# A scan with two feed-forward layers beside it: input spread between the halves of a piece, tanh ahead of bank copies, step sizes taken one tick later

## The chip, the cores and the metric

One core of a Trainium2 chip runs one program. Its engines are TensorE (PE, matmuls into PSUM), VectorE (DVE), ScalarE (ACT), GpSimd (POOL) and SyncE (SP, which here only issues DMAs). Each works through its own instructions in order and waits for the others by semaphores. The metric is the device time of one execution in microseconds, the median of several runs.

## What is computed

Four residual blocks over x of 2 x 1024 tokens and 512 features, each followed by a layer norm: linear attention, a gated feed-forward layer (with a Walsh-Hadamard transform that is folded into its second weight), a selective scan, and a second gated feed-forward layer.

```python
x = _layernorm(x + attention(x))
x = _layernorm(x + ffn0(x))          # silu(x W1) * (x W3), fwht, W2; hidden size 2048
# scan: b = 4 tiles of 512 tokens in the kernel's terms, two tiles per sequence
deltaBC = einsum('bld,od->blo', x, W_bc)          # rank 64, B 32, C 32
delta = softplus(einsum('blr,dr->bld', dt_r, W_dt) + b_dt)
h = exp(delta_t * A) * h + (delta_t * u_t) * B_t  # 512 features x 32 states
y_t = einsum('bdn,bn->bd', h, C_t);  y = y + u * D_param
x = _layernorm(x + y)
x = _layernorm(x + (silu(x Wg) * (x Wu)) Wd)      # hidden size 2048
```

## The kernel before

x stays in SBUF, features on partitions, in four tiles of 512 tokens. After the attention phase one function, `trunk_phase`, does everything else. The time axis is a count of **ticks**, from -24 to 792, that all engines walk through in their own loops (`for tick in range(FIRST_TICK, LAST_TICK)`). The same tick on two engines is not the same moment: an engine is as far as its semaphores let it be. Tables of ticks at module level say what happens in which tick.

**Feed-forward work.** Each tick has one *piece* for PE, in two halves of three matmuls (three-pass fp32: lines 84, 85, 86), `ffn(tick, 0)` and `ffn(tick, 1)`. A unit of 24 ticks makes four chunks of the hidden layer: gate (2 ticks), up (2 ticks), and the second matmul of the unit before, *down*, at ticks 2, 3, 6, 7, 10, 11, 14, 15 of the unit. One tick after a gate has ended (ticks 2, 10, 18 and 22 of a unit) ACT makes tanh of it (L1459) and DVE the silu (L1636); one tick after an up has ended DVE makes the product (L1642, "hidden"), and ACT and POOL split it one tick later into a high and a low part (L1463, L1762). Down accumulates over two ticks in PSUM bank `y_or_aux`; DVE adds it to x in the next tick (L1648).

**The scan.** 512 steps are spread over the 530 ticks from 124 to 653, one a tick (18 ticks have none). A step holds 4 features x 32 states on the 128 partitions, over 512 tokens. For step s: PE spreads delta*x from 32 rows over 128 partitions (L1386, `du_spread`, two PSUM buffers); DVE multiplies it with B (L1679, `d_b`); ACT makes `decay` = exp(delta*A) (L1553); DVE scans (L1699, `h_states`); POOL multiplies with C (L1796); PE sums the states every fourth step (L1395, `scan_y`). Every fourth step's product with B is done by POOL instead, from a copy that ACT makes (L1561, `du_copied`). In tick s DVE scans s and then makes d_b of s+1; ACT makes decay of s+1, which needs the scan of s-1; PE's spread of s+1 opens the tick and needs the d_b two steps back.

**The shared bank.** `y_or_aux` also holds what the layer norms need (mean and variance, in parts and in full), and three things of the scan's preparation for each token tile t: rank (L1340), four *dt* projections (L1351, one for each 128 features, m = 0 to 3) and two *states* matmuls (L1347, for B and C). `bank_turn(tick, half)` issues them between the pieces. The bank goes from user to user in a fixed order (`TURN`): a user waits until its predecessor's result was taken out, by ACT (a copy, or for dt an Abs and a Relu, L1524 and L1525, `dt_take`) or by DVE (the add). For tiles 1 to 3 dt comes at ticks 221, 225, 229, 233 (and 317..., 413...), that is ticks 5, 9, 13 and 17 of a unit. After the fourth, ACT makes the softplus of all four in one go (`soft`: Exp, table load, Ln, table load, L1530 to L1534), in tick 234 (330, 426).

In each tick ACT does, in this order: `copy_input` if due, decay, the bank copies that are due, tanh, h_high, and then the rest (carry, squares, splits, softplus).

## Time and profile before

| | |
|---|---|
| time, median of 3 runs | 1928.1 us (1927.26 to 1929.54) |
| profiled execution, its own time | 1931.71 us |
| its span, first to last instruction | 1929.9 us |
| mean granted TensorE clock | 0.982 |
| PE busy | 1781.0 us (92%) |
| DVE busy | 1336.6 us (69%) |
| POOL busy | 1276.2 us (66%) |
| ACT busy | 988.4 us (51%) |

The attention phase lies ahead of the trunk; the scan takes from about 584 us to 1741 us, and feed-forward work alone fills the rest. A busy share over the whole span mixes these stages, so it is read by stretches. The profile's waits name an engine, the line that waited, and what released it. A matmul's row shows 0.39 us or more, but matmuls are pipelined: in a full stream one starts every 0.23 us.

### The profile page before, as it was taken

The page shows a single profiled execution, that of the slowest core. Times are in us where ns is not written, and L with a number is a line of the kernel's source. Part 1 is how long each engine was busy: PE and PEld are TensorE (multiplying, and loading weights), DVE is VectorE, ACT ScalarE, POOL GpSimd, SP SyncE. Part 2 cuts the span into 40 slices and gives each one's busy share as a digit, 9 for nine tenths or more (in the row PEclk, how much of TensorE's full clock was granted, in tenths as well). Part 3 has the DMA queues.
Part 4 walks back from the last instruction along what each step waited for, and adds up shares of the span by engine and source line. Part 5 has one row for each costly group of instructions (what it writes and reads, how often), then busy time and mean ns, then how long its engine had stood idle before and what let it go on. Part 6 is the DMA issues. An engine that isn't in the chain of part 4 may idle for free. (4 is left out here: it accounts for less than half of the span.)

```text
span 1929.9 us, 27715 instructions
## 1 busy us (share of the span) xinstructions
PE 1781.0 (92%) x9472; PEld 1140.3 (59%) x9472; DVE 1336.6 (69%) x1665; ACT 988.4 (51%) x1671; POOL 1276.2 (66%) x987
## 2 busy tenths in 40 slices
PE   7898998679998999999899899998999999999998
PEld 5666666447855556555455455554556555566886
DVE  2525244232228999889998999889999999994222
ACT  5444342465455656565566455565665555443212
POOL 4533542137518998879887988789988898893111
PEclk9999999889999999999999999999999999999999
DMA  7342332358947888678677887667788677774653
GB/s 240 127 142 72 121 117 82 134 197 291 327 137 276 304 269 295 229 256 282 223 264 240 269 270 254 219 241 254 247 275 276 236 259 260 274 252 145 207 193 99
DMA packets 159292, 427.37 MB, mean 221 GB/s; under 512 B 30992, under 2 KB 54160, under 8 KB 158768
## 3 DMA queue, kind: packets, MB, share of 16 engines
q1 hardware_dynamic: 159152, 425.60, 65.6%
q8 instruction: 76, 1.25, 0.3%
q14 instruction: 64, 0.52, 0.1%
HBM read 356.34 MB, written 69.21 MB: 220 GB/s over the span
## 5 line engine op out<-in xcount | busy, mean ns | idle before, releaser
L1796 POOL TENSOR_TENSOR h_times_c<-h_states,c_rep 128x512 f32<-128x512 f32 x512 | 666.8, 1316 | 115.3 <-DVE h_states L1699 69.6
L1553 ACT ACTIVATE decay<-delta_on_states,a_neg 128x512 f32<-128x512 f32 x512 | 353.5, 692 | 364.6 <-DVE h_states L1699 339.1
L1762 POOL TENSOR_TENSOR h_lo<-silu_in_h_lo,h_hi 128x512 fp32r<-128x512 f32 x128 | 167.2, 1306 | 209.7 <-ACT h_hi L1463 209.1
L1679 DVE TENSOR_TENSOR d_b<-du_spread,b_rep 128x512 f32<-128x512 f32 x384 | 256.7, 668 | 24.4 <-PE du_spread L1386 23.5
L84 PE MATMUL gate<-x_hi,w 128*128 128x512 f32 x512 | 245.7, 480 | 16.4 <-DVE w L1631 6.9
L1699 DVE TENSOR_TENSOR_SCAN h_states<-decay,h_last,d_b 128x512 f32<-128x512 f32 x192 | 245.6, 1279 | 9.2 <-ACT decay L1553 2.3
L1699 DVE TENSOR_TENSOR_SCAN h_states<-decay,d_b 128x512 f32<-128x512 f32 x192 | 234.0, 1219 | 18.0 <-ACT decay L1553 11.8
L84 PE MATMUL up<-x_hi,w 128*128 128x512 f32 x512 | 241.4, 472 | 1.4 <-DVE silu_in_h_lo L1642 1.4
L1386 PE MATMUL du_spread<-stack,selectors 96*128 96x512 bf16 x512 | 201.5, 394 | 43.1 <-DVE d_b L1679 32.3
L84 PE MATMUL y_or_aux<-h_hi,w 128*128 128x512 f32 x468 | 221.0, 472 | 8.6 <-POOL h_lo L1762 6.7
L1636 DVE SCALAR_TENSOR_TENSOR silu_in_h_lo<-silu_in_h_lo,gate 128x512 f32<-128x512 f32 x128 | 87.1, 680 | 172.0 <-ACT silu_in_h_lo L1459 171.9
L85 PE MATMUL gate<-x_lo,w 128*128 128x512 f32 x512 | 203.3, 397 | 0.0
L86 PE MATMUL gate<-x_hi,w 128*128 128x512 f32 x512 | 202.8, 396 | 0.0
L85 PE MATMUL up<-x_lo,w 128*128 128x512 f32 x512 | 202.4, 395 | 0.0
L86 PE MATMUL up<-x_hi,w 128*128 128x512 f32 x512 | 201.6, 394 | 0.0
L85 PE MATMUL y_or_aux<-h_lo,w 128*128 128x512 f32 x468 | 184.4, 394 | 0.0
L86 PE MATMUL y_or_aux<-h_hi,w 128*128 128x512 f32 x468 | 184.0, 393 | 0.0
L1787 POOL TENSOR_TENSOR d_b_by_pool<-du_copied,b_rep 128x512 f32<-128x512 f32 x128 | 168.8, 1319 | 4.0 <-ACT du_copied L1561 4.0
L1386 PEld LDWEIGHTS du_spread<-stack,selectors 96*128 96x128 bf16 x512 | 49.6, 97 | 190.1 <-issue 121.4
L84 PEld LDWEIGHTS gate<-x_hi,w 128*128 128x128 f32 x512 | 99.4, 194 | 94.5 <-issue 69.9
L84 PEld LDWEIGHTS up<-x_hi,w 128*128 128x128 f32 x512 | 99.1, 193 | 75.3 <-issue 63.2
L1395 PE MATMUL scan_y<-h_times_c,sum_selectors 128*32 128x512 f32 x1024 | 139.7, 618 | 1.1 <-POOL h_times_c L1796 1.1
(221 smaller groups left out, 3134.8 us busy)
## 6 DMA issues: line engine op xcount, KB each, us to landing
w<-w_split SPq DMA_DIRECT2D x336, 512.0 KB, 4.3
delta_on_states<-delta SPq DMA_DIRECT2D x256, 512.0 KB, 5.5
w_split<-w_presplit_hi_lo SPq DMA_DIRECT2D x32, 512.0 KB, 3.3
w_split<-w SPq DMA_DIRECT2D x16, 1024.0 KB, 7.3
w_presplit_hi_lo<-in_w13b SPq DMA_DIRECT2D x32, 256.0 KB, 3.6
h_times_c<-in_w13a SPq DMA_DIRECT2D x16, 512.0 KB, 4.4
w_split<-w_presplit SPq DMA_DIRECT2D x16, 512.0 KB, 5.3
delta_x_parts<-delta_x_parts_out SPq DMA_DIRECT2D x16, 384.0 KB, 4.9
```

Of the source, the lines that this page charges most:

```text
L84: pe.matmul(out, w_hi, x_hi, start=first, stop=False)
L85: pe.matmul(out, w_hi, x_lo, start=False, stop=False)
L86: return pe.matmul(out, w_lo, x_hi, start=False, stop=last)
L1386: pe.matmul(uu[:, i % NU], sel[:, r, :], stk[:, o % 2, j]).then_inc(s_uu, 1)
L1395: mm = pe.matmul(yb[j * 32:(j + 1) * 32, :], ysel[:, r, :], hc[:, (s + j) % NC_], start=(r == 0), stop=(r == QB - 1), skip_group_check=Tru ...
L1553: act.activation(da[:, s % ND], dring[:, s % NR], ACT.Exp, scale=a[:, column(s):column(s) + 1]).then_inc(s_da, 1)
L1636: dve.scalar_tensor_tensor(out=sg[:, idx % RH], in0=sg[:, idx % RH], scalar=1.0, in1=gate[:, :], op0=ALU.add, op1=ALU.mult).then_inc(s_sg, 1)
L1679: dve.tensor_tensor(db[:, by_dve(s) % NB], uu[:, i % NU], brep[:, tile_of(s // SPO) % 2], ALU.mult).then_inc(s_db, 1)
L1699: dve.tensor_tensor_scan(hs[:, s % NH], da[:, s % ND], data, initial, ALU.mult, ALU.add).then_inc(s_hs, 1)
L1762: pool.tensor_tensor(hl[:, idx % RH], sg[:, idx % RH], hh[:, idx % RH].bitcast(F32), ALU.subtract).then_inc(s_hl, 1)
L1787: pool.tensor_tensor(dp[:, quad % 2], us[:, :], brep[:, tile_of(JB * quad // SPO) % 2], ALU.mult).then_inc(s_dp, 1)
L1796: pool.tensor_tensor(hc[:, s % NC_], hs[:, s % NH], crep[:, tile_of(s // SPO) % 2], ALU.mult).then_inc(s_hc, 1)
```

## The change

Three edits. The spread of delta*x is issued between the two halves of PE's piece, for step s+2 instead of s+1, and so stands half a tick earlier against the scan. On ACT, tanh and h_high stand ahead of the bank copies of the same tick. For tiles 1 to 3 the Abs and Relu that take a dt out of the bank are done one tick after the dt matmul (`DT_TAKE_AT`), and the two states matmuls are one tick later (235 and 237 instead of 234 and 236, and likewise for tiles 2 and 3). PE's dt matmuls, the softplus and everything on DVE, POOL and SP keep their ticks.

```diff
-STATES_TICK = ((112, 114), (234, 236), (330, 332), (426, 428))
+STATES_TICK = ((112, 114), (235, 237), (331, 333), (427, 429))
...
+DT_TAKE_AT = {tick + (key[0] > 0): key for tick, key in DT_AT.items()}
...
                     if s == -1:
                         spread_input(BY_POOL)
                         spread_input(JB + BY_POOL)
-                    if 0 <= s + 1 < STEPS and (s + 1) % JB != BY_POOL:
-                        spread_input(s + 1)
-                    if 0 <= s and s % JB == 2 and s + 2 * JB + 1 < STEPS:
-                        spread_input(s + 2 * JB + 1)
+                        spread_input(0)
                     bank_turn(tick, 0)
                     ffn(tick, 0)
+                    if -1 <= s < STEPS - 2 and (s + 2) % JB != BY_POOL:
+                        spread_input(s + 2)
+                    if s >= -1 and (s + 1) % JB == 2 and s + 2 * JB + 2 < STEPS:
+                        spread_input(s + 2 * JB + 2)
                     bank_turn(tick, 1)
...
                     if 0 <= s + 1 < STEPS:
                         decay(s + 1)
+                    if tick in TANH_AT:
+                        tanh(TANH_AT[tick])
+                    if tick in H_SPLIT_AT:
+                        h_high(H_SPLIT_AT[tick])
                     if tick in MEAN_PARTS_AT:
                         mean_parts(MEAN_PARTS_AT[tick])
...
-                    if tick in DT_AT:
-                        dt_take(*DT_AT[tick])
-                    if tick in TANH_AT:
-                        tanh(TANH_AT[tick])
-                    if tick in H_SPLIT_AT:
-                        h_high(H_SPLIT_AT[tick])
+                    if tick in DT_TAKE_AT:
+                        dt_take(*DT_TAKE_AT[tick])
```

PE around the second dt of tile 1 (ticks 225 and 226; du_spread is the spread, `y_or_aux<-h_hi` the down piece in the bank that dt used). Before:

```order
2463 L1351 MATMUL y_or_aux<-mean_or_rank,w_dt 128x512 [waits bank_taken0]
2464 L84 MATMUL gate<-x_hi,w 128x512
...
2467 L84 MATMUL gate<-x_hi,w 128x512
...
2470 L1386 MATMUL du_spread<-stack,selectors 128x512 [waits scan_db]
2471 L84 MATMUL y_or_aux<-h_hi,w 128x512 [waits w2_in2,bank_taken0]
...
2474 L84 MATMUL y_or_aux<-h_hi,w 128x512
```

and changed:

```order
2463 L1352 MATMUL y_or_aux<-mean_or_rank,w_dt 128x512 [waits bank_taken0]
2464 L84 MATMUL gate<-x_hi,w 128x512
...
2467 L1387 MATMUL du_spread<-stack,selectors 128x512 [waits scan_db]
2468 L84 MATMUL gate<-x_hi,w 128x512
...
2471 L84 MATMUL y_or_aux<-h_hi,w 128x512 [waits w2_in2,bank_taken0]
...
2474 L1387 MATMUL du_spread<-stack,selectors 128x512 [waits scan_db]
```

The spread moved from the head of the tick to its middle; the lines 85 and 86 that complete each half are left out. The wait of the down piece for the bank stands where it stood.

ACT at the same place, before (soft_in_x_hi and delta_in_x_lo are what the take writes, silu_in_h_lo is tanh):

```order
571 L1553 ACTIVATE decay<-delta_on_states,a_neg 128x512 [waits scan_h,delta_on_states1_in]
572 L1524 ACTIVATE soft_in_x_hi<-y_or_aux,scan_feat 128x512 [waits prep_dt_mm]
573 L1525 ACTIVATE delta_in_x_lo<-y_or_aux,scan_feat 128x512
574 L1553 ACTIVATE decay<-delta_on_states,a_neg 128x512 [waits scan_h]
575 L1459 ACTIVATE silu_in_h_lo<-gate 128x512 [waits y_done,gate_done]
```

and changed:

```order
571 L1555 ACTIVATE decay<-delta_on_states,a_neg 128x512 [waits scan_h,delta_on_states1_in]
572 L1555 ACTIVATE decay<-delta_on_states,a_neg 128x512 [waits scan_h]
573 L1461 ACTIVATE silu_in_h_lo<-gate 128x512 [waits y_done,gate_done]
574 L1526 ACTIVATE soft_in_x_hi<-y_or_aux,scan_feat 128x512 [waits prep_dt_mm]
575 L1527 ACTIVATE delta_in_x_lo<-y_or_aux,scan_feat 128x512
```

The take moved behind the next decay and the tanh. ACT at the fourth dt of tile 1, before:

```order
594 L1553 ACTIVATE decay<-delta_on_states,a_neg 128x512 [waits scan_h,delta_on_states2_in]
595 L1524 ACTIVATE soft_in_x_hi<-y_or_aux,scan_feat 128x512 [waits prep_dt_mm]
596 L1525 ACTIVATE delta_in_x_lo<-y_or_aux,scan_feat 128x512
597 L1553 ACTIVATE decay<-delta_on_states,a_neg 128x512 [waits scan_h]
598 L1518 COPY b_rep<-y_or_aux 128x512 [waits prep_states_mm]
599 L1459 ACTIVATE silu_in_h_lo<-gate 128x512 [waits y_done,gate_done]
600 L1565 COPY h_last<-h_states 128x2 [waits scan_h]
601 L1530 ACTIVATE soft_in_x_hi<-soft_in_x_hi 128x2048 [waits prep_abs]
```

and changed:

```order
595 L1555 ACTIVATE decay<-delta_on_states,a_neg 128x512 [waits scan_h]
596 L1461 ACTIVATE silu_in_h_lo<-gate 128x512 [waits y_done,gate_done]
597 L1526 ACTIVATE soft_in_x_hi<-y_or_aux,scan_feat 128x512 [waits prep_dt_mm]
598 L1527 ACTIVATE delta_in_x_lo<-y_or_aux,scan_feat 128x512
599 L1567 COPY h_last<-h_states 128x2 [waits scan_h]
600 L1532 ACTIVATE soft_in_x_hi<-soft_in_x_hi 128x2048 [waits prep_abs]
601 L1533 ACT_TABLE_LOAD
602 L1535 ACTIVATE soft_in_x_hi<-soft_in_x_hi 128x2048 [waits prep_exp]
603 L1536 ACT_TABLE_LOAD
604 L1563 COPY du_copied<-du_spread 128x512 [waits scan_db_by_pool,scan_du_spread]
605 L1555 ACTIVATE decay<-delta_on_states,a_neg 128x512 [waits scan_h,delta_on_states0_in]
606 L1520 COPY b_rep<-y_or_aux 128x512 [waits prep_states_mm]
```

The take stands behind tanh and right ahead of the softplus, and the copy of b_rep moved from ahead of the softplus to behind it.

## Rows read from the trace of the kernel before

**Rows 1.** By stretches: length, busy PE, PEld, DVE, ACT, POOL (instructions), clock, DMA, GB/s.

```profile
787.00:834.00 47.00, 41.98 (x161) 22.54 (x161) 35.52 (x44) 31.22 (x53) 33.25 (x27) 0.93 0.63 210
...
1269.00:1740.00 471.00, 448.86 (x2058) 265.22 (x2057) 456.10 (x531) 259.23 (x448) 416.74 (x325) 1.00 0.77 259
```

**Rows 2.** Waits of DVE, 577 to 1740 us: total, times, longest.

```profile
DVE silu_in_h_lo L1636 <- ACT silu_in_h_lo L1459: 28.2, 19, 10.2
DVE d_b L1679 <- PE du_spread L1386: 23.5, 31, 1.8
DVE h_states L1699 <- ACT decay L1553: 15.4, 10, 5.2
```

**Rows 3.** Waits of PE, same stretch.

```profile
PE du_spread L1386 <- DVE d_b L1679: 32.3, 35, 3.8
```

**Rows 4.** Waits of DVE, 787:834, 1011:1053, 1227:1269; then PE's, 787:817.

```profile
DVE d_b L1679 <- PE du_spread L1386: 2.5, 3, 1.1
...
DVE d_b L1679 <- PE du_spread L1386: 4.1, 6, 1.4
...
DVE d_b L1679 <- PE du_spread L1386: 5.1, 6, 1.2
...
PE y_or_aux L1351 <- DVE x L1648: 1.3, 1, 1.3
```

**Rows 5.** Timeline at the second dt, PE and then ACT: start, duration, what, [idle before].

```profile
797.24 1.12 PE L1351 MATMUL y_or_aux<-mean_or_rank,w_dt 64*128 64x512 f32 x2
...
799.56 0.39 PE L86 MATMUL gate<-x_hi,w 128*128 128x512 f32 x1
799.79 0.39 PE L1386 MATMUL du_spread<-stack,selectors 96*128 96x512 bf16 x1
799.83 0.59 PE L84 MATMUL y_or_aux<-h_hi,w 128*128 128x512 f32 x1
...
798.40 0.69 ACT L1524 ACTIVATE soft_in_x_hi<-y_or_aux,scan_feat 128x512 f32<-128x512 f32 x1 [2.71 <-PE y_or_aux L1351]
798.99 0.68 ACT L1525 ACTIVATE delta_in_x_lo<-y_or_aux,scan_feat 128x512 f32<-128x512 f32 x1
```

**Rows 6.** Timeline at the first dt, DVE and then PE.

```profile
788.16 1.22 DVE L1699 TENSOR_TENSOR_SCAN h_states<-decay,d_b 128x512 f32<-128x512 f32 x1
...
790.90 0.58 PE L84 MATMUL y_or_aux<-h_hi,w 128*128 128x512 f32 x1
```

**Rows 7.** Timeline at the softplus, by engine; last, stretch 827 to 830 us as in rows 1.

```profile
817.65 0.39 PE L1386 MATMUL du_spread<-stack,selectors 96*128 96x512 bf16 x1
...
820.19 1.93 ACT L1530 ACTIVATE soft_in_x_hi<-soft_in_x_hi 128x2048 f32<-128x2048 f32 x1
...
827.13 1.31 ACT L1553 ACTIVATE decay<-delta_on_states,a_neg 128x512 f32<-128x512 f32 x2
...
827.86 1.22 DVE L1699 TENSOR_TENSOR_SCAN h_states<-decay,d_b 128x512 f32<-128x512 f32 x1 [5.20 <-ACT decay L1553]
...
827.29 0.61 PE L1386 MATMUL du_spread<-stack,selectors 96*128 96x512 bf16 x1 [3.77 <-ACT du_copied L1561]
...
827.00:830.00 3.00, 2.71 (x4) 0.77 (x5) 2.14 (x3) 1.50 (x4) 2.10 (x2) 0.50 0.00 0
```

**Rows 8.** Timeline at the longest wait for a spread, DVE and then ACT.

```profile
1502.96 0.69 DVE L1679 TENSOR_TENSOR d_b<-du_spread,b_rep 128x512 f32<-128x512 f32 x1 [1.79 <-PE du_spread L1386]
1503.57 0.68 DVE L1636 SCALAR_TENSOR_TENSOR silu_in_h_lo<-silu_in_h_lo,gate 128x512 f32<-128x512 f32 x1
...
1502.75 0.60 ACT L1459 ACTIVATE silu_in_h_lo<-gate 128x512 f32<-128x512 f32 x1
```

**Rows 9.** Timeline where a variance copy stands ahead of tanh, ACT and then DVE.

```profile
1202.00 0.60 ACT L1479 ACTIVATE rstd<-y_or_aux 128x512 f32<-128x512 f32 x1 [1.34 <-PE y_or_aux L1326]
1202.50 0.59 ACT L1459 ACTIVATE silu_in_h_lo<-gate 128x512 f32<-128x512 f32 x1
...
1203.12 0.69 DVE L1636 SCALAR_TENSOR_TENSOR silu_in_h_lo<-silu_in_h_lo,gate 128x512 f32<-128x512 f32 x1 [0.71 <-ACT silu_in_h_lo L1459]
```

## The prediction

> **What bounds the kernel now.** I read the table by stretches first. The scan of the third layer fills 577 to 1740 us. From 1269 to 1740 us VectorE (DVE) is busy for 456.1 of 471 us and TensorE (PE) for 448.9 at full clock [rows 1]: two engines, each nearly full, and whichever is late makes the other wait. The stretch 787 to 834 us is different: DVE is busy for only 35.5 of 47 us there. It is one of three stretches (787 to 834, 1011 to 1053, 1227 to 1269) in which the step sizes of the next token tile are made.
>
> Then the waits. Over the stage DVE waits 23.5 us for du_spread in 31 places, 28.2 us for tanh (10.2 of it in one piece before the first scan) and 15.4 us for decay [rows 2]. PE waits 32.3 us for d_b in 35 places [rows 3], since du_spread has two buffers. Of the 23.5 us, the three stretches hold 2.5 + 4.1 + 5.1 = 11.7 us [rows 4], which leaves 11.8 us for the rest of the scan.
>
> Then one tick inside a size stretch, in the timeline. The projection to step sizes (dt, L1351) starts at 797.24, both halves of a gate piece follow, and at 799.83 PE starts a down piece into the same PSUM bank, y_or_aux. That works because ScalarE (ACT) emptied the bank at 798.40 and 798.99, at once [rows 5]. From 787 to 817 us PE has one wait, 1.3 us [rows 4], so PE is the bound between the four dt of a tile. The softplus behind the fourth holds ACT from 820.19, and DVE sits for 5.20 us until decay can follow it at 827.13 [rows 7]. So in a size stretch the chain is PE, dt, ACT, softplus, decay, scan; whatever delays the fourth take delays the scan.
>
> **The change, part by part.** The kernel's profiled execution took 1931.71 us for a span of 1929.9 us; the median of the runs is 1928.1. I work out differences from the profile and add them to the median.
>
> *Step sizes taken a tick behind (tiles 1 to 3).* Abs and Relu of a dt now stand behind the next tick's decay, and after tanh where that tick has one. PE's down piece of that next tick still needs the bank. This concerns three of four dt of a tile (m = 0, 1, 2, ticks 221, 225, 229 and the like); the fourth has no down piece right behind it.
> - m = 0: the scan at 788.16 lasts 1.22, so decay can start at 789.5, Abs and Relu each 0.6 behind (the spacing of 798.40 and 798.99 [rows 5]), Relu lasts 0.68, and PE is let go near 791.5. It went at 790.90 [rows 6]. Cost 0.6 us.
> - m = 1: this tick has a tanh, which needs the gate piece that PE is just ending. Its last matmul starts at 799.56 and is over when the next starts, about 0.23 later. The spread now lies inside the piece, so the gate ends 0.25 later (a tick's spread moved forward, not added). Tanh near 800.2, Abs 800.8, Relu 801.4, bank free near 802.1, against 799.83 [rows 5]. Cost 2.3 us, in which PE has nothing it may start.
> - m = 2: PE is 2.9 us behind by then, and DVE not, so decay is early and the take is done in time. Cost 0.
> - m = 3: taken behind a tanh and a decay, but the copy of b_rep leaves the queue ahead of the softplus. The gate piece ended at 817.65, where the next spread starts, and now ends near 817.65 + 2.9 + 0.25 = 820.8; tanh, Abs and Relu at 0.6 each put Exp near 822.7, where it was at 820.19 [rows 7]. So the softplus, and the scan behind it, is 2.5 us later.
>
> The takes wait less for PE, since dt is done when ACT comes to it, but DVE waits in these stretches for PE and for the softplus, so ACT's own waits bring nothing. The 11.7 us that DVE waits for du_spread there don't count as a gain either: what it wins, it waits at the softplus. Three tiles at 2.5 us: **+7.5 us**. Bounds: 0 if the PE time given up is made good before the fourth dt, 3 x 3.5 = 10.5 if m = 2 costs too.
>
> Here the Trainium skill (Perfetto Trace Analysis, Matmuls under Optimizing Tensor Performance) speaks against the change: matmul groups should rotate through banks so that the emptying of one overlaps the matmuls of the next. Here dt and down share one bank, and the change lengthens its emptying; by that rule alone every one of the nine takes would stall PE. The rows give a stall at six.
>
> *States a tick later, and the restart.* b_rep is now copied behind the softplus, and the second states matmul waits for it; the copied du of that tick is waited for at the middle of PE's tick instead of the next one's start. PE idled 3.77 us there and came back at half the clock for 827 to 830 us [rows 7]. It now stops half a tick sooner, with 0.7 to 1.5 us more to do after the stop, part of it slow. DVE finds it late in one tile of three as I read it: **+1.0 us** (0 to 2.5).
>
> *The spread half a tick sooner.* A du_spread costs PE the same inside a piece as ahead of it. What moves is the phase. Before, PE's spread for step s+1 opens tick s and needs the d_b of s-1; now the one for s+2 stands in the middle and needs the d_b of s. A tick takes 2.2 us on average (1163 us for 530), the half piece ahead of the spread 0.7 us (three matmuls at 0.23): DVE may run about 1.5 us further ahead of PE before it waits for a spread, and PE may run 1.5 us less ahead of DVE. DVE also waits for PE through tanh, and that limit does not move. The longest wait for du_spread shows it: 1.79 us to 1502.96, then the gate's silu at 1503.57. The tanh that silu needs starts at 1502.75 and lasts 0.60 [rows 8], so with an early spread DVE stops at the silu instead until 1503.4: 0.2 of 1.79 us gained. The other waits above 1 us outside the size stretches include one more of this kind. Where only a hidden product or an add follows, most of the wait is won. I take 30% of 11.8 us: **-3.5 us** (0 to -11.8).
>
> *Tanh ahead of bank copies.* It moves where a tick has both a tanh and a mean or variance copy. At 1202.00 ACT waited 1.34 us for PE's variance parts, then tanh at 1202.50, then DVE's silu after 0.71 us [rows 9]. In four ticks outside the size stretches such a silu waits; the copy ahead lasts 0.5 to 0.6. **-1.5 us** (0 to -2.2). The copies go 0.6 later and nobody is near them.
>
> *Ends.* At the last scan PE stands less far ahead and the rest is PE's: **+0.5 us** (0 to 1.5). Sum: 7.5 + 1.0 - 3.5 - 1.5 + 0.5 = +4.0 us, **1932.1 us**.
>
> **The rivals.**
> 1. The waits go, all of them. DVE is the fuller engine over most of the stage [rows 1]; if silus and hidden products are mostly ready when the spread is early, the whole 11.8 and 2.2 us are won, against the same 7.5: -6.5, 1921.6 us. For it: many waits are under 1 us. Against: [rows 8].
> 2. The lead is what counts (slower). PE's lead shrinks by 1.5 us, so after any tick with aux matmuls the gate piece comes late and DVE waits at tanh instead. If this turns the 3.5 us of gain into none and the restarts cost their 2.5: 7.5 + 2.5 - 1.5 + 0.5 = +9, 1937.1 us. It decides if DVE's wait for tanh grows beyond the 28.2 us of [rows 2] by more than that for du_spread shrinks.
> 3. The bank stall does not reach the scan: PE idles 2.3 us, but had it to spare since it also waits 32.3 us for d_b [rows 3]. Against: it has one wait of 1.3 us in the stretch concerned [rows 4]. Then -3.5 - 1.5 + 1 + 0.5 = -3.5, 1924.6 us.
> 4. Nothing moves, as the tables of ticks shift waits but not their sum: 1928.1 us.
>
> **How the numbers follow.** Forecast 0.40, spread over 1929 to 1936; rival 1 0.20; rival 2 0.17; rival 3 0.13; rival 4 0.10. The range that holds 8 in 10 takes rival 1 in at its figure and rival 2 with the bound of 10.5 for the takes: 1921 to 1940 us. The forecast's own range is 1928 to 1937. A measurement tells 0.2% (3.9 us) from no change: slower means above 1932.0. The forecast lies on that line, so half of it and rival 2 are slower, some of the bounds with them: 0.43. Faster: rival 1 and half of rival 3: 0.27. Same: 0.30.
>
> **What would show it.** In the profile after: a wait of PE's down piece (y_or_aux, L84) for the Relu of the take, about 2 us in three places and about 0.6 in three; ACT's wait ahead of Abs nearly gone; Exp of the softplus about 2.5 us later against the first dt of its tile; PE's stop at the softplus longer. Outside, waits of DVE for du_spread near zero, and those for tanh not smaller by as much. It would be wrong if no wait at the down pieces appears, if it appears and DVE's total idle time in the three stretches is unchanged, or if the waits for du_spread vanish without others in their place.

## The result, and the profile after

The changed kernel takes **1944.18 us** (median of 8 runs, 1938.93 to 1951.74); the kernel before, on the same chip, 1930.53 us (median of 8). The ratio is 1.0069 with a 95% interval of 1.0046 to 1.0092: **slower by 0.7%**, 13.6 us. The forecast was 1932.1 us and the range ended at 1940. The profiled execution took 1940.18 us of its own time, its span is 1938.4 us; the numbers of before were 1931.71 and 1929.9. The profile thus shows 8.5 us of the 13.6. The forecast was worked out from a kernel before of 1928.1 us, and the eight runs beside the changed kernel put it at 1930.5, so the difference, +13.6 us against a forecast +4.0, is the fair comparison.

The work is the same: busy times from the page of the changed kernel.

```profile
PE 1780.6 (92%) x9472; PEld 1145.7 (59%) x9472; DVE 1332.3 (69%) x1665; ACT 988.7 (51%) x1671; POOL 1278.6 (66%) x987
```

So the time is in waits. DVE's over 577 to 1740 us, changed kernel (total, times, longest), to be held against [rows 2]:

```profile
DVE silu_in_h_lo L1638 <- ACT silu_in_h_lo L1461: 39.1, 30, 10.2
DVE h_states L1701 <- ACT decay L1555: 24.1, 14, 6.4
DVE d_b L1681 <- PE du_spread L1387: 9.1, 11, 2.0
DVE silu_in_h_lo L1644 <- PE up L86: 7.6, 7, 2.4
```

The wait for the spread fell from 23.5 to 9.1 us. The waits for tanh rose from 28.2 to 39.1, for decay from 15.4 to 24.1, and those for the up piece (L1644) from 1.1 to 7.6. What was saved at the spread came back at other instructions, and about 12 us more.

PE's waits over the same stretch, against [rows 3]:

```profile
PE du_spread L1387 <- DVE d_b L1681: 31.1, 43, 3.2
PE du_spread L1387 <- ACT du_copied L1563: 28.2, 19, 5.5
PE y_or_aux L84 <- ACT delta_in_x_lo L1527: 5.7, 4, 1.8
PE y_or_aux L1348 <- ACT b_rep L1520: 3.8, 2, 2.1
```

The third row is the bank: down pieces that wait for the Relu of a late take. The second is new in its size. A spread into the second buffer after a spread for POOL has to wait until ACT has copied that one out (`du_copied`); before, PE waited for it twice, 9.3 us, both behind a softplus (5.5 of it ahead of the first scan).

Timeline at the second dt of the first size stretch (start, duration, what, [idle before]), the place of [rows 5]:

```profile
798.36 1.12 PE L1352 MATMUL y_or_aux<-mean_or_rank,w_dt 64*128 64x512 f32 x2
...
801.34 0.60 ACT L1461 ACTIVATE silu_in_h_lo<-gate 128x512 f32<-128x512 f32 x1 [1.96 <-PE gate L86]
801.84 0.68 ACT L1526 ACTIVATE soft_in_x_hi<-y_or_aux,scan_feat 128x512 f32<-128x512 f32 x1
...
802.41 0.69 ACT L1527 ACTIVATE delta_in_x_lo<-y_or_aux,scan_feat 128x512 f32<-128x512 f32 x1
...
803.15 0.50 PE L84 MATMUL y_or_aux<-h_hi,w 128*128 128x512 f32 x1 [1.84 <-ACT delta_in_x_lo L1527]
```

Gate ends, tanh, Abs, Relu, and only then PE's down piece: the chain of the prediction's step m = 1. The same row with the same 1.84 stands at 1033.57 and at 1250.25, once for each later tile. From the start of the first dt of a tile to its Exp it is 33.9, 35.5 and 33.3 us, where it was 31.9, 32.4 and 31.8: 2.0, 3.2 and 1.4 later.

At the softplus, the timeline of the changed kernel, against [rows 7]:

```profile
823.05 1.93 ACT L1532 ACTIVATE soft_in_x_hi<-soft_in_x_hi 128x2048 f32<-128x2048 f32 x1
...
825.00 1.28 ACT L1533 ACT_TABLE_LOAD   x1
826.29 1.91 ACT L1535 ACTIVATE soft_in_x_hi<-soft_in_x_hi 128x2048 f32<-128x2048 f32 x1
...
830.15 0.61 PE L1387 MATMUL du_spread<-stack,selectors 96*128 96x512 bf16 x1 [5.00 <-ACT du_copied L1563]
...
830.72 1.22 DVE L1701 TENSOR_TENSOR_SCAN h_states<-decay,d_b 128x512 f32<-128x512 f32 x1 [6.36 <-ACT decay L1555]
```

and its stretch 830 to 833 us (length, busy PE, PEld, DVE, ACT, POOL, granted clock, DMA, GB/s):

```profile
830.00:833.00 3.00, 2.85 (x10) 0.75 (x11) 1.81 (x2) 2.59 (x6) 0.20 (x1) 0.50 0.00 0
```

The scan waits 6.36 us instead of 5.20, PE 5.00 instead of 3.77, and PE comes back at a granted clock of 0.50, which is 1.2 GHz.

**Where along the scan it was lost.** From the starts of DVE's scan instructions (one for each step) I take the time since the scan of step 0 and subtract the same of the kernel before. The experiments below are in the table with it. Each line is one execution, and eight runs of one kernel lie up to 13 us apart, so a step in one line counts only where other lines repeat it.

```
us against before     step 16    32    96   112   192   208   272   288   511
changed kernel          +2.1  +6.7  +4.4  +7.9 +11.3 +14.6  +9.9 +12.3 +11.8
a_spread                +2.3  +6.5  +5.6  +6.7 +11.3 +11.1  +6.9  +8.8  +8.7
b_tanh                  +0.3  +1.1  +0.4  -0.2  +1.1  +0.6  -4.1  -4.0  +1.2
c_take                  +2.4  +2.1  +0.8  -2.0   0.0  -0.1  -3.6  -3.6  -3.5
g_no_take               -0.9  +6.8  +5.3  +8.7 +11.7 +11.0  +8.6  +8.9  +7.1
h_no_spread             +0.1  +1.2  +0.9  +1.6  +3.8  +6.5  +1.8  +3.7  +3.4
e_copy                  +0.8  +3.4  +3.2  +9.9 +15.4 +17.1 +11.5 +15.5 +13.1
f_sp                     0.0  +5.8  +3.0  +7.5 +10.4 +12.2  +8.4 +10.8 +10.8
s_take_first            -0.3  +6.4  +5.1  +5.1  +8.8  +7.5  +2.6  +2.9  +1.8
w_all_but_spread        +0.1  +0.7  +0.6  -1.6  +0.4  +0.9  -4.7  -4.7  -3.1
u_from_48               -0.2  +0.4  -0.2  -0.6  +2.8  +1.6  -1.2  -0.8  -4.7
v_from_208              -0.5  +1.3  -0.3  -2.5  -0.2  +0.3  -5.9  -5.6  -6.7
m_phase_early           +1.0 +10.9 +14.1 +16.8 +23.3 +24.1 +22.4 +28.0 +35.1
n_phase_late            -0.3  +0.8  +2.1  +2.3  +9.7 +11.1  +5.7  +8.3 +20.2
```

The size stretches of the three tiles lie at steps 96 to 112, 192 to 208 and 272 to 288. The changed kernel loses 3.5, 3.3 and 2.4 us in them. But its largest single loss comes between steps 16 and 32, far ahead of the first late take. That isn't in the prediction at all. It is no accident of one execution: at step 32 five kernels whose spread is half a tick sooner from the start (the changed one, a_spread, g_no_take, s_take_first, f_sp) stand at +5.8 to +6.8, and the eight that don't have it sooner in these steps (t_late_tanh with them, +1.3) at +0.4 to +2.1.

Two things in the table belong to the single execution of the kernel before. Between steps 208 and 272 every version gains on it, by 1.7 to 6.2 us, also those with the spread at its old place: the kernel before lost time there, and no edit gained any. And the first scan starts at 586.5 us before and at 583.2 in the changed kernel (581.3 to 587.4 over all traces, in no order that the edits explain); so of the 11.8 us lost in the scan the profiled execution shows 8.5, and nothing is lost behind the scan.

### The profile page after: what moved, and what is told of

It is laid out like the page before. It is cut to its first block and busy times, and to the rows that moved or that the text cites. A ratio compares the mean times of both kernels' runs of the same rounds, so it can differ in the third digit from the quotient of the medians.

```text
span 1938.4 us, 27715 instructions
## 1 busy us (share of the span) xinstructions
PE 1780.6 (92%) x9472; PEld 1145.7 (59%) x9472; DVE 1332.3 (69%) x1665; ACT 988.7 (51%) x1671; POOL 1278.6 (66%) x987
## 5 line engine op out<-in xcount | busy, mean ns | idle before, releaser
L84 PE MATMUL gate<-x_hi,w 128*128 128x512 f32 x512 | 244.5, 477 | 12.2 <-DVE w L1633 7.1
L84 PE MATMUL up<-x_hi,w 128*128 128x512 f32 x512 | 235.2, 459 | 1.1 <-DVE silu_in_h_lo L1644 1.1
L84 PE MATMUL y_or_aux<-h_hi,w 128*128 128x512 f32 x468 | 216.2, 462 | 9.1 <-ACT delta_in_x_lo L1527 5.7
L86 PE MATMUL up<-x_hi,w 128*128 128x512 f32 x512 | 200.8, 392 | 0.0
L86 PE MATMUL y_or_aux<-h_hi,w 128*128 128x512 f32 x468 | 183.7, 393 | 0.0
L84 PEld LDWEIGHTS gate<-x_hi,w 128*128 128x128 f32 x512 | 99.8, 195 | 88.6 <-issue 62.6
L84 PEld LDWEIGHTS up<-x_hi,w 128*128 128x128 f32 x512 | 98.1, 192 | 74.7 <-issue 61.4
```

Source lines behind the costliest of these rows:

```text
L84: pe.matmul(out, w_hi, x_hi, start=first, stop=False)
L86: return pe.matmul(out, w_lo, x_hi, start=False, stop=last)
```

## Experiments

Each ratio is to the kernel before on the same chip (1930.9 to 1932.0 us in the four sets), with its 95% interval; "own time" is that of the one profiled execution.

| kernel | median us | ratio | own time us |
|---|---|---|---|
| a_spread | 1939.84 | 1.0049 [1.0033, 1.0064] | 1940.72 |
| b_tanh | 1929.43 | 0.9988 [0.9974, 1.0002] | 1930.71 |
| c_take | 1929.38 | 0.9990 [0.9975, 1.0006] | 1923.58 |
| g_no_take (spread, tanh) | 1933.72 | 1.0012 [0.9997, 1.0027] | 1933.55 |
| h_no_spread (tanh, take) | 1937.52 | 1.0022 [1.0007, 1.0036] | 1934.56 |
| s_take_first | 1931.30 | 0.9999 [0.9986, 1.0012] | 1933.80 |
| w_all_but_spread | 1927.36 | 0.9982 [0.9968, 0.9996] | 1926.92 |
| e_copy | 1945.43 | 1.0078 [1.0058, 1.0099] | 1944.68 |
| f_sp | 1942.24 | 1.0055 [1.0037, 1.0074] | 1941.79 |
| q_copy_sp | 1940.53 | 1.0044 [1.0023, 1.0065] | 1940.57 |
| m_phase_early | 1970.16 | 1.0191 [1.0165, 1.0217] | 1965.85 |
| n_phase_late | 1957.32 | 1.0144 [1.0122, 1.0166] | 1948.26 |
| t_late_tanh | 1952.60 | 1.0114 [1.0094, 1.0134] | 1950.69 |
| u_from_48 | 1927.53 | 0.9983 [0.9969, 0.9997] | 1927.89 |
| v_from_208 | 1926.24 | 0.9970 [0.9957, 0.9983] | 1923.73 |

### The three edits, each alone

a_spread is the kernel before with the spread moved, and nothing else:

```diff
-                    if 0 <= s + 1 < STEPS and (s + 1) % JB != BY_POOL:
-                        spread_input(s + 1)
...
                     ffn(tick, 0)
+                    if -1 <= s < STEPS - 2 and (s + 2) % JB != BY_POOL:
+                        spread_input(s + 2)
```

> The kernel before with the spread between the halves alone; tanh, takes and states as before. Theory 1 (the spread in the middle of the piece needs ACT's copy of du half a tick sooner, and PE stops for it: 28.2 us in 19 places after the change, 9.3 in 2 before): this alone costs most of the difference, +6 to +11 us, and PE's waits for du_copied rise above 20 us. Theory 2 (the late take of the step sizes is the cost): -4 to +1 us, with DVE's waits for du_spread near 9 us and du_copied waits not mattering.

b_tanh moves tanh and h_high ahead of the bank copies:

```diff
                         decay(s + 1)
+                    if tick in TANH_AT:
+                        tanh(TANH_AT[tick])
+                    if tick in H_SPLIT_AT:
+                        h_high(H_SPLIT_AT[tick])
```

> The kernel before with tanh and h_high ahead of ACT's bank copies alone. Both theories: -2 to 0 us, the four silus behind a variance copy wait 2 us less in all. A rise of over 2 us would speak for a third cause: bank copies that came too late.

c_take takes the step sizes a tick later, with the states matmuls a tick later too. The take stands where it stood in its tick, ahead of tanh:

```diff
-                    if tick in DT_AT:
-                        dt_take(*DT_AT[tick])
+                    if tick in DT_TAKE_AT:
+                        dt_take(*DT_TAKE_AT[tick])
                     if tick in TANH_AT:
                         tanh(TANH_AT[tick])
```

> The kernel before with the Abs and Relu one tick behind for tiles 1 to 3 and the states matmuls a tick later, alone; tanh stays behind the bank copies. Theory 2: +5 to +9 us, PE's down pieces wait for the Relu. Theory 1: +1 to +4 us, since here the take is ahead of tanh and needs no gate; the softplus starts up to 1 us later a tile.

Measured: +0.49%, -0.12% and -0.10%. a_spread and b_tanh came out as expected; c_take missed both theories, which had it slower by at least 1 us. Added up that is +0.27%, and all together +0.69%: the edits aren't independent. The spread, to which the prediction had given a gain of 3.5 us, costs 9.5 us by itself (0.49% of 1931). Its waits, 577 to 1750 us:

```profile
DVE silu_in_h_lo L1637 <- ACT silu_in_h_lo L1460: 46.4, 32, 10.2
PE du_spread L1386 <- DVE d_b L1680: 42.7, 52, 3.2
ACT decay L1554 <- DMA delta_on_states<-delta: 34.3, 19, 6.1
PE du_spread L1386 <- ACT du_copied L1562: 27.8, 20, 5.7
DVE h_states L1700 <- ACT decay L1554: 20.0, 14, 5.2
DVE silu_in_h_lo L1643 <- PE up L86: 6.0, 7, 1.8
DVE d_b L1680 <- PE du_spread L1386: 3.3, 5, 0.9
```

DVE's wait for the spread is down to 3.3 us, which is what the edit is able to do. Over this longer stretch the kernel before waits 32.1 us for tanh, but 3.9 of that is a wait behind the last scan, which in a_spread lies outside the stretch (at 1756.9). Held against the 28.2 without it, tanh is up by 18.2, decay by 4.6 and the up piece (1.1 before) by 4.9, together 27.7 against the 20.2 saved. The difference of 7.5 us is close to the 8.7 us by which the scan is longer.

### Pairs, and the place of the take

g_no_take is the changed kernel without the late take and the later states; h_no_spread is the changed kernel without the spread's move. Their edits are the hunks shown above, combined.

> The change without the late take: spread between the halves and tanh first. Alone the spread cost 8.9 us and the late take 1.6 less than nothing, all three 13.6. If the parts add up: +7 us against before. If the late take costs 4 to 6 us only together with the spread: +7 to +9 here, and the kernel without the spread (next) near 0. PE's waits at the down pieces for ACT are absent.

> The change without its spread: tanh first and the late take behind it, so the down piece of three ticks waits for gate, tanh, Abs and Relu. The prediction's term for this was +7.5 us less 1.5. Rival theory (additive single parts): -3 us. Third (PE has a lead over VectorE that the spread took away, and which covers the bank wait): 0 to +2 us with waits of PE at the down pieces under 2 us in all.

By the ratios the late take costs 0.57% on spread and tanh (changed kernel against g_no_take) and 0.34% on tanh alone (h_no_spread against b_tanh), but nothing when it was alone. (For g_no_take I had expected +7 to +9 us and it is +2.3; h_no_spread at +4.3 fell between its theories and nearest to the prediction's +6.) In c_take there is no wait of a down piece for Relu; in h_no_spread there is:

```profile
PE y_or_aux L84 <- ACT delta_in_x_lo L1526: 5.2, 5, 1.6
```

The difference is that c_take has the take ahead of tanh. s_take_first is the changed kernel with that order:

```diff
                         decay(s + 1)
+                    if tick in DT_TAKE_AT:
+                        dt_take(*DT_TAKE_AT[tick])
                     if tick in TANH_AT:
                         tanh(TANH_AT[tick])
...
-                    if tick in DT_TAKE_AT:
-                        dt_take(*DT_TAKE_AT[tick])
```

> The changed kernel with the late take moved ahead of tanh and h_high on ACT (as it stood when the take alone was changed); the rest of the change stays. Theory 'a take that is late costs only because tanh stands ahead of it': PE's waits of the down piece for Relu, 5.7 us in 4 places in the changed kernel, fall to 1 us or less, and the time comes down to about that of the changed kernel without the late take, 1932 to 1937. Rival 'the late take costs wherever it stands, because the softplus moves': 1940 to 1945 with the waits of the down piece gone but the softplus gaps of DVE (6.4 us at the first tile) unchanged.

It takes 1931.30 us, as fast as the kernel before, and 12.9 us less than the changed kernel. The waits for Relu are down to one of 0.2 us. In the table along the scan the two part by 3.5 us at steps 96 to 112, 4.6 at 192 to 208 and 2.1 at 272 to 288, 10.2 in all, and run in parallel from 288 on. That is one mechanism in three places, though the first isn't clean: g_no_take, without any late take, loses 3.4 us between steps 96 and 112 too. It came out just under what I expected (1932 to 1937).

w_all_but_spread is s_take_first with the spread back at the head of the tick.

> Tanh and h_high ahead of the bank copies, late take with the take ahead of tanh, states a tick later; the spread stays where it was before. With s_take_first (ratio 0.9999) it is the pair that differs in the spread alone. Theory 'the spread half a tick sooner costs mostly in its first 32 steps': this one is 0.2 to 0.35% faster than s_take_first, 1924 to 1928. Theory 'the spread is neutral once tanh stands right': within 0.1% of it, 1929 to 1933.

0.9982 against 0.9999: with tanh and the take in good order, the spread still costs 0.17%, 3.3 us (the intervals overlap a little: 0.9968 to 0.9996 and 0.9986 to 1.0012). It cost 0.24% on tanh first (g_no_take against b_tanh) and 0.49% on nothing. The other way round: tanh first is worth 0.12% alone and 0.37% once the spread is early (a_spread against g_no_take). An early spread leaves tanh as the place where DVE meets PE, and then what stands ahead of tanh on ACT counts. That reading is argued from the waits; the numbers show only that the edits depend on each other.

### Two suspects for the early spread's cost

The trace of the changed kernel showed two new or longer stops: PE's for `du_copied` (28.2 us) and decay's for the delta loads (34.2 us, 22.6 before). e_copy has ACT copy the spread for POOL a tick sooner; f_sp has SP issue the delta loads first in its tick; q_copy_sp has both. All keep the rest of the change.

```diff
-                    if 0 <= s < STEPS and s % JB == BY_POOL and s // JB + 2 < STEPS // JB:
+                    if 0 <= s < STEPS and s % JB == 2 and s // JB + 2 < STEPS // JB:
```

```diff
                     s = step_at(tick)
+                    if s >= 0 and s % 2 == 1 and s + NR - 1 < STEPS:
+                        delta_load((s + NR - 1) // 2)
```

> All of the change, and ACT copies du one step sooner (s % 4 == 2 instead of 3), so that the copy is done before PE's next spread in the middle of a piece. Theory 1: PE's waits for du_copied fall from 28.2 to below 12 us and 5 to 9 us of the 13.6 come back. Theory 2: within 2 us of the changed kernel. If the waits fall and the time does not, the stops of PE were covered and theory 1 falls.

> All of the change, and SyncE issues the delta loads ahead of the weight loads of their tick. Theory 3 (PE runs later against VectorE, so weight loads in SyncE's queue wait longer for PE and hold up the delta loads behind them; decay waits 34.2 us for them, 22.6 before): decay's waits for the load fall below 20 us and 5 us or more come back. If the waits fall and less than 2 us come back, or they do not fall, it is not the queue's order.

> The changed kernel with both stops taken away that looked suspicious in its trace: ACT copies the spread for POOL one tick earlier (at turn 2 of 4 instead of 3) and SP issues the delta loads first in its tick. Alone they gave 1945.4 and 1942.2 where the changed kernel had 1944.2. Theory 'these stops are only where the lost lead shows': 1940 to 1946, with the waits for du_copied under 10 us and those of decay for delta under 10 us. Theory 'each stop hid the other': 1933 to 1938.

Both edits do what they are for, and neither brings the time back: e_copy is at 1.0078 and f_sp at 1.0055, where the changed kernel is at 1.0069, with intervals that overlap. PE's waits in e_copy, 577 to 1750 us, and decay's wait in f_sp:

```profile
PE du_spread L1387 <- DVE d_b L1681: 43.1, 63, 3.2
...
PE y_or_aux L84 <- ACT delta_in_x_lo L1527: 9.6, 6, 2.2
...
PE du_spread L1387 <- ACT du_copied L1563: 8.1, 6, 5.3
```

```profile
ACT decay L1555 <- DMA delta_on_states<-delta: 7.2, 4, 2.4
```

In e_copy PE waits 20 us less for the copy, but 12 us more for d_b and 4 us more for Relu. In f_sp the stop moved to a weight load that now comes later:

```profile
630.31 0.63 ACT L1451 ACTIVATE w_presplit<-w_presplit 128x512 f32<-128x512 f32 x1 [3.96 <-DMA w_presplit<-in_w2b]
...
632.98 0.61 PE L1387 MATMUL du_spread<-stack,selectors 96*128 96x512 bf16 x1 [6.04 <-ACT du_copied L1563]
```

So f_sp doesn't clear late loads of blame: one late load took the place of another. What it does show is that the total of decay's waits for delta isn't the cost. h_no_spread waits 31.5 us for them with the spread at its old place, and v_from_208, the fastest of all, 33.4.

q_copy_sp, with both waits under 10 us (9.0 and 6.5), is at 1.0044 [1.0023, 1.0065] where the changed kernel is at 1.0069 [1.0046, 1.0092]. The intervals overlap; by the middles, a quarter of a per cent may hang on the two stops together, and most of the loss doesn't.

### The phase, in both directions

m_phase_early moves the spread of s+2 to the head of the tick, so another half tick sooner. n_phase_late leaves it at s+1 but in the middle of the tick, half a tick later than before. t_late_tanh is n_phase_late with tanh first.

```diff
-                    if 0 <= s + 1 < STEPS and (s + 1) % JB != BY_POOL:
-                        spread_input(s + 1)
...
+                        spread_input(0)
+                    if -1 <= s < STEPS - 2 and (s + 2) % JB != BY_POOL:
+                        spread_input(s + 2)
...
                     bank_turn(tick, 0)
                     ffn(tick, 0)
```

```diff
-                    if 0 <= s + 1 < STEPS and (s + 1) % JB != BY_POOL:
-                        spread_input(s + 1)
...
                     bank_turn(tick, 0)
                     ffn(tick, 0)
+                    if 0 <= s + 1 < STEPS and (s + 1) % JB != BY_POOL:
+                        spread_input(s + 1)
```

> The kernel before with the spread of s+2 at the head of tick s: half a tick sooner still than in the change, at the place where no piece is split. Theory 4 (what counts is how far PE may run ahead of VectorE; each half tick sooner takes 0.7 to 1.5 us of it): +14 to +20 us against before, more than the +8.9 of the spread alone; VectorE's waits for tanh above 50 us. If it is the splitting of the piece that costs: 0 to +5 us.

> The kernel before with only one edit: the spread of step s+1 moves from the head of tick s to its middle, half a tick LATER against the scan (the spread of the changed kernel went half a tick sooner, two versions back a whole tick sooner). Both engines are coupled by two buffers, so the phase fixes how far PE may be ahead of DVE. Theory 'PE's lead is what counts': PE may now run half a tick further ahead; its waits for d_b fall from 32.3 us to under 25, DVE's for tanh stay at or below 32 (28.2 to 32.1 before), DVE's for du_spread rise from 23.5 to 35 or more. If lead counted alone the time would fall below 1931; I expect the two sides about even, 1926 to 1940. Theory 'half way is an optimum whatever the direction': the same size of loss as sooner, 1938 to 1942. Theory 'the lead of DVE is what counts' (the prediction's): slower, at least 3.5 us, with tanh waits unchanged.

> The kernel before with tanh and h_high ahead of the bank copies and the spread of s+1 in the middle of tick s (half a tick later instead of sooner). Against the run with tanh first alone (1929.4) it gives the third point of the phase on that basis: theory 'PE's lead counts': 1925 to 1931; theory 'the place at the head of the tick is best': 1933 to 1940. The waits for tanh should be at or under 28 us, those for du_spread over 35 us.

A tick sooner costs 1.91%, half a tick sooner 0.49%, half a tick later 1.44%. The first was a miss in size, 37 us where I had 14 to 20, with 67.1 us of wait for tanh; it refutes that the splitting of the piece costs, since nothing is split there. It also rules out the clock as what carries the loss: the mean granted clock of its profiled execution is 0.984, where the kernel before has 0.982. The last was a clear miss: I had expected at most 1940 us for n_phase_late and it took 1957, and t_late_tanh missed in the same way. The theory that PE's lead alone counts is refuted by it. DVE's waits, and then PE's, of n_phase_late over 577 to 1750 us:

```profile
DVE d_b L1679 <- PE du_spread L1386: 59.9, 62, 3.0
DVE silu_in_h_lo L1636 <- ACT silu_in_h_lo L1459: 19.0, 10, 10.2
...
PE gate L84 <- DVE silu_in_h_lo L1636: 14.9, 14, 1.9
PE y_or_aux L84 <- DVE x L1648: 14.5, 13, 2.7
PE y_or_aux L1351 <- DVE x L1648: 11.9, 12, 1.7
PE du_spread L1386 <- DVE d_b L1679: 9.8, 17, 1.3
```

(The wait for tanh behind the last scan, 3.9 us, lies outside this stretch here; the 19.0 go against 28.2.) Now DVE waits for the spread, and PE, whose wait for d_b fell from 32.3 to 9.8 us, waits for DVE at the other tiles that they share: the gate banks (L84 behind the silu), and `y_or_aux` behind the add. The two engines share several buffers. The phase sets which of these is the tightest, and on either side one of them pays; that is how I read these waits, and no run took one of the buffers away.

### Where the early spread costs: switching the phase in mid-scan

u_from_48 and v_from_208 are s_take_first with the spread at the head of the tick up to a step, and half a tick sooner from there on (48 in the first, 208 in the second):

```diff
-                        spread_input(0)
+                    if 0 <= s + 1 < STEPS and s <= 48 and (s + 1) % JB != BY_POOL:
+                        spread_input(s + 1)
+                    if 0 <= s <= 48 and s % JB == 2:
+                        spread_input(s + 2 * JB + 1)
                     bank_turn(tick, 0)
                     ffn(tick, 0)
-                    if -1 <= s < STEPS - 2 and (s + 2) % JB != BY_POOL:
+                    if 48 <= s < STEPS - 2 and (s + 2) % JB != BY_POOL:
                         spread_input(s + 2)
-                    if s >= -1 and (s + 1) % JB == 2 and s + 2 * JB + 2 < STEPS:
+                    if s >= 48 and (s + 1) % JB == 2 and s + 2 * JB + 2 < STEPS:
```

> As s_take_first, but the spread goes half a tick sooner only from step 48 on; for steps 0 to 48 it opens the tick as before. In s_take_first the scan lost 6.4 us against the kernel before between steps 16 and 32 (cumulative time of the scans) and gained 4.6 us after. Theory 'the loss is made in the first 32 steps, where ACT's copy for POOL and the delta loads are late': the step at 16 to 32 is gone, the rest stays, 1924 to 1928. Theory 'two engines that are both full settle at the same time wherever the phase changes': 1929 to 1933, a loss appears elsewhere.

> As u_from_48 with the change of phase at step 208, just ahead of the second half of the scan, where all versions with the early spread gained 3 to 5 us against the kernel before (steps 208 to 272). Theory 'which phase is better depends on the stretch': 1923 to 1927, the best of all. Theory 'no stretch really gains, the gain is what was lost before': no better than w_all_but_spread, within 0.1% of it.

u_from_48 is at 0.9983, the same as w_all_but_spread (0.9982), which never moves the spread. What the spread costs in s_take_first (0.16%, 3.1 us, against u_from_48, with intervals that overlap a little; 5.9 us by own times) is made in the first 48 steps; from there on half a tick makes no difference that these runs can tell. The step of 6.4 us at 16 to 32 is gone from its row in the table. In s_take_first it is made at two places: 2.5 us at step 22, after a first late load (626.9 us), and 4.1 at steps 26 to 29. How the second is made, in the timeline of s_take_first and then its stretch 650 to 655 us (columns as above):

```profile
647.94 0.69 ACT L1555 ACTIVATE decay<-delta_on_states,a_neg 128x512 f32<-128x512 f32 x1 [4.57 <-DMA delta_on_states<-delta]
...
650.31 0.57 ACT L1563 COPY du_copied<-du_spread 128x512 f32<-128x512 f32 x1
...
650.94 0.39 PE L1387 MATMUL du_spread<-stack,selectors 96*128 96x512 bf16 x1 [1.63 <-ACT du_copied L1563]
...
656.45 0.60 ACT L1461 ACTIVATE silu_in_h_lo<-gate 128x512 f32<-128x512 f32 x1 [4.25 <-PE gate L86]
...
657.09 0.69 DVE L1638 SCALAR_TENSOR_TENSOR silu_in_h_lo<-silu_in_h_lo,gate 128x512 f32<-128x512 f32 x1 [3.17 <-ACT silu_in_h_lo L1461]
```

```profile
650.00:655.00 5.00, 4.06 (x17) 2.17 (x17) 3.92 (x5) 2.21 (x6) 4.61 (x4) 0.76 0.85 316
```

The same steps and stretch in u_from_48:

```profile
645.27 0.69 ACT L1558 ACTIVATE decay<-delta_on_states,a_neg 128x512 f32<-128x512 f32 x1 [3.11 <-DMA delta_on_states<-delta]
...
647.64 0.57 ACT L1566 COPY du_copied<-du_spread 128x512 f32<-128x512 f32 x1
...
650.81 0.60 ACT L1464 ACTIVATE silu_in_h_lo<-gate 128x512 f32<-128x512 f32 x1 [1.02 <-PE gate L86]
...
651.76 0.67 DVE L1641 SCALAR_TENSOR_TENSOR silu_in_h_lo<-silu_in_h_lo,gate 128x512 f32<-128x512 f32 x1
```

```profile
650.00:655.00 5.00, 5.00 (x24) 3.74 (x22) 4.91 (x7) 2.52 (x5) 5.00 (x5) 1.00 0.94 355
```

A delta load comes late and ACT stands for 3 to 5 us in both. With the spread at the head PE never stops in this stretch, and DVE is busy for 4.91 of 5 us. With the spread half a tick sooner PE reaches it before ACT has made the copy, stops for 1.63 us, and the granted clock falls to 0.76 in that stretch; the gate is late, so is tanh, and DVE waits 3.17 us. One late DMA is passed on from ACT to PE to DVE. The load itself is later in s_take_first (a wait of 4.57 against 3.11 us), so this pair alone doesn't tell the late load from PE's lead. e_copy does. There ACT waits 4.72 us for the same load, but its copy stands a tick sooner, and this is PE's stop and the stretch behind it:

```profile
649.03 0.39 PE L1387 MATMUL du_spread<-stack,selectors 96*128 96x512 bf16 x1 [0.72 <-ACT du_copied L1563]
...
650.00:655.00 5.00, 5.00 (x25) 3.51 (x21) 5.00 (x7) 2.78 (x7) 4.82 (x4) 1.00 0.86 301
```

PE stops for 0.72 us, the clock stays at 1.00, DVE is busy throughout, and the 3.3 us of step 29 aren't lost; e_copy stands at +3.4 at step 32. q_copy_sp, which has the same edit, loses 0.9 us at that step. So at this place PE's stop for the copy is what passes the late load on. e_copy isn't faster as a whole because it loses more later on, 6.7 us between steps 96 and 112 alone; PE waits 9.6 us for Relu in it.

v_from_208 is the fastest of all, 0.9970 [0.9957, 0.9983], 1926.24 us: faster than both kernels. Against w_all_but_spread (0.9982) the 0.12% is inside both intervals, so whether the later half of the scan gains from the early spread stays open. What is shown is that it doesn't lose.

## Why the prediction was wrong

**The sum, edit by edit.** By the ratios, in the order tanh, spread, take with states: -2.3 (b_tanh), +4.6 (g_no_take against it), +11.0 (the changed kernel against that), together 13.3 us. The prediction had -1.5, -3.5, and 7.5 + 1.0. The spread is off by 8.1 us and the take by 2.5, so the spread is where the prediction failed, and the take's term is second.

**The late take, +7.5: right in mechanism and place, too small beside the other edits.** The stall of the down piece is there at m = 1 of all three tiles, 1.84 us each where I had 2.3. At m = 0 I had 0.6 us each and the trace has one small wait at most (5.7 us in 4 places, three of them 1.84), at m = 2 none, as forecast. From the first dt to Exp the three tiles are 2.0, 3.2 and 1.4 us longer, 6.6 in all where I had 7.5. The scan gives back 10.2 us in the size stretches once the take stands ahead of tanh, and the whole kernel 13.5 us by the ratios (0.70%); without the early spread the late take costs 6.6 us (0.34%). So 7.5 was about right for the take by itself, and 3.5 to 6 us short with the early spread around it; why the two edits add to each other is argued above and not shown. Rival 3, that the stall doesn't reach the scan, is refuted. The Trainium skill (Perfetto Trace Analysis, Matmuls) has matmul groups rotate through banks so that emptying one overlaps the next; the nine takes that share a bank with down gave three stalls of 1.84 us and at most one of 0.2, and with the take ahead of tanh none above 0.2, so the order on ACT and not the sharing alone decided them.

**States and restart, +1.0: not found as a cost.** PE's stop at the softplus is longer (5.00 against 3.77 us), as is its wait ahead of L1348 (3.8 us in 2 places). But c_take and w_all_but_spread have the later states as well and lose nothing.

**The spread, -3.5 (0 to -11.8): the step that failed.** I took the waits for du_spread, asked what else DVE would wait for in their place, and kept 30% as gain. I bounded the term at 0 on the bad side, since "DVE may run further ahead" looked as if it could only help. The same sentence said that PE may run 1.5 us less ahead, and the sum gave that no price (rival 2 named it, and let it do no more than cancel the gain). It has one, +9.5 us alone, 3.3 to 4.6 with tanh first. The bound should have come from a place where ACT is late and PE isn't, and the trace of before had it: ACT waited 3.44 us for a delta load at 644.28 and PE, busy for all of 640 to 655 us, didn't stop. What covered it was PE's lead, and the edit took half a tick of that away. In the changed kernel ACT waits 6.81 us at this place and PE stops for 2.43.

```profile
644.28 0.69 ACT L1553 ACTIVATE decay<-delta_on_states,a_neg 128x512 f32<-128x512 f32 x1 [3.44 <-DMA delta_on_states<-delta]
```

**Rival 2 came nearest, with two corrections.** It said that PE's lead counts and gave 1937.1 us. Its chance was 0.17. It put the loss behind ticks with aux matmuls and at zero gain; what the early spread costs with tanh and the take in good order is in the first 48 steps, behind stops of ACT such as late loads. And its sign (tanh's wait grows by more than the spread's shrinks) would have misled: in a_spread tanh's grew by 18.2 and the spread's shrank by 20.2. Only with decay and the up piece is the sum positive, and u_from_48 waits 39.0 us for tanh, where the kernel before waits 32.1 over the same stretch, and is faster than before:

```profile
DVE silu_in_h_lo L1641 <- ACT silu_in_h_lo L1464: 39.0, 24, 10.2
...
DVE d_b L1684 <- PE du_spread L1387: 5.8, 9, 1.1
```

**Tanh first, -1.5: right alone** (-0.12%, 2.3 us, the interval reaches just past no change), but it is also what puts tanh ahead of the take. The prediction had both edits in one sum of single terms, with this coupling inside the take's term. **Rivals 1 and 4** fall with the measured time. **Ends, +0.5:** nothing is lost behind the scan.

What stays open: why the late take costs more under an early spread; why half a tick later costs as much as 1.44% in detail (the trace names the shared buffers, no run took one of them away), and whether v_from_208's lead over w_all_but_spread is real. Its expectation rested on a gain behind step 208 that belongs to the one trace of the kernel before, as said under the table, so there is less reason for it than I then thought.

## What to carry to other kernels

When two full engines are coupled by a ring of two buffers, moving one's place in its loop takes lead from one to give it to the other: price both sides, and look for the places where a third engine is held up and this lead is what hides it. A move of a wait should be tried by stretches, since here the loss that was left once tanh and the take stood in good order came from the first 48 of 512 steps. And before a step in one trace is read as a gain, see whether every version shows it: then it is the baseline's. When a result is emptied later, ask which instruction of the same engine stands ahead of the emptying and what *it* waits for: the same late take cost about 13 us behind a tanh that waits for PE, and nothing ahead of it.

## What was unexpected of the hardware

After PE stood still for 5.00 us the granted clock was 0.50 over 830 to 833 us, and after a stop of 1.63 us (s_take_first) it was 0.76 over 650 to 655 us. By single microseconds that is full speed first and half speed later:

```profile
651.00:652.00 1.00, 1.00 (x9) 0.19 (x9) 1.00 (x3) 1.00 (x2) 1.00 (x2) 1.00 0.85 348
...
654.00:655.00 1.00, 1.00 (x5) 0.48 (x3) 0.00 (x0) 0.00 (x0) 1.00 (x2) 0.50 0.86 344
```

From 652.59 to 655.60 the matmuls of the gate start 0.43 us apart instead of 0.23. So a stop of under 2 us can be paid for a second time, but it need not be: behind the stops of 1.84 us at the down pieces of the changed kernel the clock stayed at 1.00 at 803 and 1250 us, and fell to 0.50 over 1035 to 1037 us behind the one at 1033 us.

The two table loads of the softplus take 1.28 us each, and Ln starts at 826.29, right as the first load (from 825.00) ends. The Trainium skill (ScalarE: Activation LUTs, What ACT_TABLE_LOAD costs) gives 2.66 us a switch, of which 1.38 are a drain. The load agrees; the drain isn't to be seen here, as Exp ends at 824.98 and the load starts at 825.00.
